# Second residual of the attention block added by TensorE in the feed-forward's bank instead of by VectorE

## The chip, the cores and the metric

One Trainium2 chip, one of its cores. The metric is the device time of one execution in microseconds (us), the median of three runs. The core's engines each work through a program of their own in order and meet by semaphores: TensorE (PE, matmuls), VectorE (DVE), ScalarE (ACT), GpSimd (POOL, which here also issues scattered DMAs) and SyncE (SP, DMA issue).

## What is computed

A transformer block on x of shape (2, 2048, 128): Performer attention with 16 heads, then a mixture of 8 experts with top-2 routing and one shared expert, each with its norms and residuals.

```python
h = _performer_attn(x, wq, wk, wv, wo, omega)
x = _layernorm(x + h, ln1_g, ln1_b)
h2 = gelu(x @ w1 + b1) @ w2 + b2
x = _layernorm(x + h2, ln2_g, ln2_b)          # the addition x + h2 is what the change moves
...
x = x + _layernorm(attention_block(_layernorm(x)))
x = x + _layernorm(experts(_layernorm(x)))     # top-2 of 8, and a shared expert
```

## The kernel before

The 4096 rows are cut into NG = 8 groups of 512 rows (n = 0 to 7; GB = 4 of them are one batch). A group lies in SBUF as 128 partitions by 4 tiles of 128 features. Three parts follow each other: attention features and the sums of the first batch (to about 175 us), a software pipeline over the eight groups (to about 404 us), and 39 blocks of expert work with a closing norm.

The change lies in the pipeline. `pipeline(stage)` makes each engine's program: for every step it goes through the groups n = 0 to 7, and group n is at its stage k = step - 2n + 5. So a group starts two steps after the one before, within a step the elder group comes first, and what an engine does for different groups is interleaved in a fixed order. A group's stages that matter here, with "(n)" for the group:

- k = 1, 2: for n >= 4 only, the division of the attention: PE turns the denominators (L698), DVE takes reciprocals (L1195), ACT spreads them (L931), PE turns them back (L705, waits for ACT), DVE multiplies (L1201, "divide"), and PE's next group of L691 waits for that.
- k = 4, 5: first residual (L1205), statistics, and first norm N1 (L1088 into MID) on DVE; PE turns N1 into the bank pT (L592).
- k = 6: ACT makes X1T = g * N1T + b on the turned side (L990, with the gains per partition). DVE makes the same x2 = g * N1 + b + b2 on the unturned side with two steps (L1255, L1257) into XN.
- k = 7: PE up projection (L778), ACT gelu (L995).
- k = 8: PE down projection into the bank pQKV, "down(n)" (L785, 16 matmuls, each of two passes). It waits for s_r2 of the group before, that is for DVE's L1275 having read the bank.
- k = 9: DVE adds x2 and the bank into R2 (L1275), takes statistics (L1077, L1081) from R2; POOL makes 1/sqrt and -mean times that (L437, L441, L503, L506).
- k = 10, 12: ACT normalises, "norm2(n)" out of R2 and then "norm3(n)" out of the result NY (both L970, four of 128 x 128 each).
- k = 11, 13, 14: DVE gain and bias (L1281, L1283), residual (L1288), last norm "norm4(n)" (L1088 into PL), of which ACT makes a copy (L986).
- k = 15 to 19: routing; k = 20, 21: POOL scatters the group's rows to DRAM with 8 indirect DMAs (L489). In its order the first of them stands behind the L506 of norm2(5).
- k = 23 to 27: the shared expert, which uses pQKV too.

What stands behind what on the in-order engines matters: in step 2n+3, PE has (in this order) down(n), turn back of the reciprocals of group n+3, the sums L691 of group n+4; and ACT has the copy L986 of group n-3, norm3(n-2), norm2(n-1) and X1T(n+1).

Of the kernel before, what the change touches and what calls it, by code (L numbers as in the profile page):

```python
# [38 lines left out]
ALU = mybir.AluOpType  # L39
# [3 lines left out]
P = 128  # L43
# [36 lines left out]
def build(nc, xs, ys, x, wqkv, wqkT, omT, wo, cols, rows, w1, w2, ew1T, ew2T, gwT, out):  # L80
# [4 lines left out]
    with ExitStack() as ctx:  # L85
# [15 lines left out]
        WH = sb("WH", [P, WA], F32R)  # L101
        WL = sb("WL", [P, WA], F32R)
        wo_s = sb("wo_s", [P, P])
        cols_s = sb("cols_s", [P, 2 + FC])
        rows_s = sb("rows_s", [P, 5, P])
        b12 = sb("b12", [P, P])
        w1_s = sb("w1_s", [P, FF])
        w2_s = sb("w2_s", [P, FC, P])
        gwT_s = sb("gwT_s", [P, E])
# [36 lines left out]
        ATX = sb("ATX", [P, 2, GW])  # L146
        ATT, X1T = ATX[:, 0, :], ATX[:, 1, :]
        MID = sb("MID", [P, 5, GW])
        N1, R2 = (MID[:, i, :] for i in range(1, 3))
        NY = [MID[:, 3, :], MID[:, 4, :]]  # L150
        HT = sb("HT", [P, FC, GW])
        XFH = sb("XFH", [P, GB, GW], F16)
# [56 lines left out]
        def parts(flat, *widths):  # L209
# [49 lines left out]
        s_num, s_nb, s_dt, s_rd = sem("den_num"), sem("den_num_copied"), sem("den_turned"), sem("den_recip")  # L259
        s_rdx, s_rx, s_att, s_wo, s_r1 = (  # L260
            sem("recip_spread"), sem("recip_turned"), sem("attn"), sem("wo_done"), sem("res1"))
        s_nT, s_x1t, s_up, s_ge, s_dn, s_r2 = (sem(n) for n in (
            "n1_turned", "x1t", "up_done", "gelu_done", "down_done", "res2"))
        s_n2g, s_y2, s_x1 = sem("n2_times_g"), sem("y_ready"), sem("x1_ready")
        s_fT, s_xft, s_xfh, s_xfl, s_lg, s_lgc = (sem(n) for n in (
            "xf_turned", "xf_copied", "xf_hi", "xf_lo", "logits", "logits_copied"))
# [3 lines left out]
        s_rt, s_place, s_base, s_slot = (sem(n) for n in (  # L270
            "routed", "placing_step", "base_next", "slots"))
        s_scat = [sem(f"scattered{g}") for g in range(GB)]
        s_n1g, s_x2 = sem("n1_times_g"), sem("x2_ready")
        s_free, s_spare = sem("rows_sent"), sem("spare_written")
        s_tab, s_fil, s_fill = sem("table_step"), sem("filler_rows_step"), sem("fillers_written")
        s_ssq, s_sc = sem("w1_squares_summed"), sem("scale_step")
# [60 lines left out]
        @block.sync  # L337
        def _(sp):
            sp.dma_start(X[:, 0, :], x_v[0]).then_inc(s_x[0], 16)
            sp.dma_start(omT_s, omT).then_inc(s_wq, 16)  # L340
            sp.dma_start(wqkT_s, wqkT).then_inc(s_wq, 16)
            sp.dma_start(W_f, wqkv).then_inc(s_wq, 16)
            sp.dma_start(X[:, 1, :], x_v[1]).then_inc(s_x[1], 16)
            sp.dma_start(EW1.rearrange("p (e h) -> p e h", e=E + 1), ew1T).then_inc(s_ew1, 16)
            sp.dma_start(rows_s[:].rearrange("p v d -> p (v d)"), rows.to_broadcast([P, 5 * P])).then_inc(s_w, 16)
            sp.dma_start(cols_s[:], cols).then_inc(s_w, 16)
            sp.dma_start(gwT_s[:], gwT).then_inc(s_w, 16)
            sp.dma_start(wo_s[:], wo).then_inc(s_w, 16)
            sp.dma_start(w1_s[:], w1).then_inc(s_w, 16)
            sp.dma_start(w2_s[:], w2).then_inc(s_w, 16)  # L350
            for g in range(2, GB):
                sp.dma_start(X[:, g, :], x_v[g]).then_inc(s_x[g], 16)
            for g in range(GB):

                sp.wait_ge(s_x[g], 16)
                sp.dma_start(X[:, GB + g, :], x_v[GB + g]).then_inc(s_x[g], 16)
            sp.dma_start(E2[:], ew2T).then_inc(s_w2, 16)

            sp.wait_ge(s_fil, 2)
            for g in range(2):  # L360
                n = SPARE // 2
                sp.dma_start(xs[E * CAP + g * n:E * CAP + (g + 1) * n].rearrange("(p a) w -> p a w", p=P),
                             SPR[:, g * n // P:(g + 1) * n // P]).then_inc(s_spare, 16)
            for b in range(B):
                for m in range(E // B):

                    if b == 0:
                        sp.wait_ge(s_batch, 1)
                    else:
                        sp.wait_ge(s_el, m + 2)  # L370
                    w = ew1T[:, bass.ds(b * (E // B) + m + 1, 1), :].rearrange("p e h -> p (e h)")
                    sp.dma_start(W1S[:, m, :], w).then_inc(s_stage[m], 16)

            sp.wait_ge(s_fil, 4)
            sp.wait_ge(s_tab, 2)
            for e in range(E):
                row = sp.value_load(filslot[0:1, e:e + 1], min_val=0, max_val=XROWS - BW)
                sp.dma_start(xs[bass.ds(row, BW)].rearrange("(p a) w -> p a w", a=2), FIL[:, e]).then_inc(s_fill, 16)

            sp.wait_ge(s_fill, 16 * E)  # L380
            for g in range(GB):
# [12 lines left out]

            for n in range(NG):
                sp.dma_start(YC[n], ys_v[n]).then_inc(s_bx[n], 16)
# [3 lines left out]
        def _(pool):  # L400
# [132 lines left out]
            rstd(0, 1)  # L533
            eng.memset(PL[:].rearrange("p g t a w -> p (g t a) w")[:, :, D:RW], 0.0).then_inc(s_free, 1)
            pool.wait_ge(s_w, 16 * NLOADS)
            eng.tensor_tensor(b12[:], rows_s[:, 1, :], rows_s[:, 2, :], ALU.add).then_inc(s_const, 1)
            pool.wait_ge(s_const, NCONST + 1)
            pool.wait_ge(s_prep_v, NPREP)
            n = SPARE // 2
# [42 lines left out]
        def _(pe):  # L582
# [170 lines left out]
            def stage(n, g, k):  # L753
# [14 lines left out]
                if k == 5:  # L768
                    pe.wait_ge(s_no[1], n + 1)

                    wait(pe, s_x1t, n)
                    turn(pT, lambda t: N1[:, t * P:(t + 1) * P]).then_inc(s_nT, 1)
                if k == 7:
                    pe.wait_ge(s_x1t, n + 1)
# [3 lines left out]
                        nc.tensor.matmul(pPK[c % 2][:], w1_s[:, c * P:(c + 1) * P], X1T,  # L778
                                         start=True, stop=True).then_inc(s_up, 1)
                if k == 8:  # L780
                    wait(pe, s_r2, n)
                    pe.wait_ge(s_ge, (n + 1) * FC)
                    for t in range(T):
                        for c in range(FC):
                            m = nc.tensor.matmul(pQKV[:, t * P:(t + 1) * P], HT[:, c, t * P:(t + 1) * P],  # L785
                                                 w2_s[:, c, :], start=(c == 0), stop=(c == FC - 1))
                    m.then_inc(s_dn, 1)
                if k == 15:
                    pe.wait_ge(s_no[4], n + 1)
# [33 lines left out]
                              [XFH[:, g], XFL[:, g]]).then_inc(s_su, 1)  # L823
                if k == SHARED + 3:

                    pe.wait_ge(*((s_sh, n) if n else (s_r2, NG)))
# [63 lines left out]
        def _(act):  # L890
# [83 lines left out]
            def stage(n, g, k):  # L974
                if k == 10:
                    if n >= 2:
                        act.wait_ge(s_x1, n - 1)
                    norm_act(2, n, R2)
                if k == 12:
                    norm_act(3, n, NY[n % 2])  # L980
                if k == 1 and n >= GB:
# [5 lines left out]
                if k == 6:  # L987
                    wait(act, s_up, n * FC)
                    act.wait_ge(s_nT, n + 1)
                    A(X1T, pT[:], ACT.Identity, scale=cols_s[:, 0:1], bias=cols_s[:, 1:2]).then_inc(s_x1t, 1)  # L990
                if k == 7:
                    wait(act, s_dn, n)
                    for c in range(FC):
# [66 lines left out]
        def _(dve):  # L1060
# [183 lines left out]
            def stage(n, g, k):  # L1244
                if k == 5:
                    if n == 0:
                        dve.wait_ge(s_spare, 16 * 2)
                    wait(dve, s_nT, n)
                    wait(dve, s_n1g, n)
                    norm(1, n, tiles(N1), XN[:, n])  # L1250
                if k == 6:

                    dve.wait_ge(s_no[1], n + 1)
                    x2, n1 = (u.rearrange("p (t d) -> p t d", t=T) for u in (XN[:, n], N1))
                    v.tensor_tensor(x2, n1, rows_s[:, 0, :].unsqueeze(1).to_broadcast([P, T, D]), ALU.mult).then_inc(s_n1g, 1)  # L1255
# [13 lines left out]
                if k == 4 and n >= GB:  # L1269
                    res1(n, pPQ)  # L1270
                if k == 9:
                    wait(dve, s_no[2], n)
                    dve.wait_ge(s_x2, n + 1)
                    dve.wait_ge(s_dn, n + 1)
                    v.tensor_tensor(R2, pQKV[:], XN[:, n], ALU.add).then_inc(s_r2, 1)  # L1275
                    hold(s_r2, n + 1)
                    stats(2, n, R2)
                if k == 11:
                    dve.wait_ge(s_no[2], n + 1)
                    y = NY[n % 2].rearrange("p (t d) -> p t d", t=T)  # L1280
                    v.tensor_tensor(y, y, rows_s[:, 3, :].unsqueeze(1).to_broadcast([P, T, D]), ALU.mult).then_inc(s_n2g, 1)  # L1281
                    dve.wait_ge(s_n2g, n + 1)
                    v.tensor_tensor(y, y, rows_s[:, 4, :].unsqueeze(1).to_broadcast([P, T, D]), ALU.add).then_inc(s_y2, 1)  # L1283
                    hold(s_y2, n + 1, at=3)
                    stats(3, n, NY[n % 2])
                if k == 13:
# [191 lines left out]
```

## Time and profile before

| what | value |
|---|---|
| median of 3 runs | 598.88 us (595.96 to 599.67) |
| the profiled execution | 594.31 us, span of its instructions 592.6 us |
| PE busy | 460.4 us (78%) |
| DVE busy | 316.1 us (53%) |
| ACT busy | 261.4 us (44%) |
| POOL busy | 245.2 us (41%) |
| chain that ended last | PE 58%, DVE 14%, POOL 8%, issue 7%, ACT 5% |

Busy shares are averages over parts with different limits; the second table of the page cuts the span into 40 slices of 14.8 us, and a digit is the busy share in tenths. The pipeline is slices 12 to 27.

### The profile page before, as it was taken

How to read it: one execution, taken by the hardware profiler on the slowest of the kernel's cores; microseconds unless marked ns; L12 is line 12 of the kernel's file. 1: busy time of each engine (PE TensorE's matmuls, PEld its weight loads, DVE VectorE, ACT ScalarE, POOL GpSimd, SP SyncE). 2: the span in 40 equal slices, each digit the busy share in tenths (PEclk: the TensorE clock that was granted, in tenths of full speed). 3: DMA queues.
4: the chain of work that ended last, by engine and by line, in shares of the span. 5: the costliest groups of instructions: out<-in, count | busy, mean ns of one | idle time of the engine just before them, and what ended most of it. 6: DMA issues, size and time to landing. Idle time of an engine off the chain costs nothing.

```text
span 592.6 us, 10592 instructions
## 1 busy us (share of the span) xinstructions
PE 460.4 (78%) x3392; PEld 355.3 (60%) x3392; DVE 316.1 (53%) x1298; ACT 261.4 (44%) x540; POOL 245.2 (41%) x368
## 2 busy tenths in 40 slices
PE   3899999999979888867727657598999999997000
PEld 2577766676655555656514435377989888987000
DVE  6887785786573578799865312301322222222394
ACT  2655544445434566644734213234445444443053
POOL 7300000110001134237887775500655555656592
PEclk9999999999998999987978777788999999999555
DMA  8920010000000000000001111330222222221622
GB/s 271 359 71 19 6 32 1 2 2 1 2 0 1 0 2 1 2 1 19 28 33 43 47 55 37 102 83 1 69 82 74 73 74 73 77 65 38 244 108 88
DMA packets 17843, 33.88 MB, mean 57 GB/s; under 512 B 4128, under 2 KB 10528, under 8 KB 17536
## 3 DMA queue, kind: packets, MB, share of 16 engines
q1 hardware_dynamic: 12096, 21.68, 11.4%
q0 software_dynamic: 4544, 9.45, 4.8%
q10 hardware_dynamic: 1152, 2.10, 0.9%
q8 instruction: 29, 0.48, 0.3%
q14 instruction: 22, 0.18, 0.1%
HBM read 19.65 MB, written 13.56 MB: 56 GB/s over the span
## 4 chain that ended last, share of the span: by engine, by line
PE 58%; DVE 14%; POOL 8%; issue 7%; ACT 5%; another core or an unknown queue 4%; DMA 2%; SPq 0%; POOLq 0%; DVEq 0%; ACTq 0%
PE pQKV L869 6%; PE pF L587 5%; POOL xs L489 4%; PE pPK L585 3%; PE pPK L587 3%; PE pPK L586 3%; PE pKV L662 3%; PE pF L585 3%; PE pQKV L831 3%; PE pPQ L869 3%; PE pF L586 3%; PE pQKV L785 2%; PE pPK L778 2%; PE pF L691 2%
## 5 line engine op out<-in xcount | busy, mean ns | idle before, releaser
L437 POOL TENSOR_TENSOR ve<-mv,eps 128x4 f32<-128x4 f32 x40 | 9.5, 238 | 209.3 <-DVE mv L1081 208.9
L556 POOL DMA_INDIRECT ys<-MID,PQT x78 | 76.0, 974 | 24.8 <-issue 24.8
L489 POOL DMA_INDIRECT xs<-PL,SLOT x64 | 64.1, 1001 | 20.0 <-issue 20.0
L1395 DVE TENSOR_SCALAR MID<-pQKV,PQT 128x128 f32<-128x128 f32 x40 | 12.2, 347 | 83.6 <-remote 66.4
L441 POOL TENSOR_TENSOR rs<-ve,halves 128x4 f32<-128x4 f32 x40 | 42.5, 1061 | 3.1
L869 PE MATMUL pQKV<-E,HT 128*128 x320 | 39.1, 275 | 1.2 <-ACT HT L1037 1.2
L585 PE MATMUL pPK<-XFH,E1H 128*128 128x512 f16 x32 | 15.3, 478 | 31.6 <-ACT MID L1015 15.3
L869 PEld LDWEIGHTS pQKV<-E,HT 128*128 128x128 f32 x320 | 37.3, 192 | 1.6 <-issue 1.4
L869 PE MATMUL pPQ<-E,HT 128*128 x304 | 37.3, 276 | 0.6 <-DVE MID L1395 0.6
L430 POOL TENSOR_TENSOR held<-halves 128x1 f32<-128x1 f32 x47 | 9.2, 195 | 67.7 <-DVE MID L1395 57.9
L869 PEld LDWEIGHTS pPQ<-E,HT 128*128 128x128 f32 x304 | 35.5, 192 | 1.2 <-issue 0.9
L778 PE MATMUL pPK<-ATX,w_s 128*128 128x512 f32 x64 | 32.9, 641 | 3.6 <-ACT HT L995 1.8
L1153 DVE TENSOR_REDUCE MX<-pPK 128x16 f32<-128x512 f32 x32 | 21.8, 682 | 24.7 <-PE pPK L587 24.6
L785 PE MATMUL pQKV<-w_s,HT 128*128 128x128 f32 x256 | 33.5, 294 | 0.3 <-ACT HT L995 0.3
L785 PEld LDWEIGHTS pQKV<-w_s,HT 128*128 128x128 f32 x256 | 32.2, 208 | 0.6 <-ACT HT L995 0.6
L995 ACT ACTIVATE HT<-pPK,cols_s 128x512 f32<-128x512 f32 x32 | 21.8, 689 | 21.9 <-PE pPK L778 20.9
L1027 ACT ACTIVATE PK<-pKV 128x256 f16<-128x256 f32 x19 | 7.3, 384 | 54.3 <-PE pF L587 47.8
L1037 ACT ACTIVATE HT<-pPK,wunscale 128x512 f32<-128x512 f32 x38 | 24.8, 687 | 11.7 <-PE pPK L587 8.6
L1387 DVE TENSOR_TENSOR PK<-pT,PK 128x256 f16<-128x256 f32 x20 | 8.5, 425 | 37.8 <-ACT PK L1027 37.5
L909 ACT ACTIVATE PK<-pPK 128x512 f32<-128x512 f32 x32 | 19.2, 600 | 20.4 <-PE pPK L645 20.4
L585 PEld LDWEIGHTS pPK<-XFH,E1H 128*128 128x128 f16 x32 | 3.8, 119 | 40.5 <-ACT MID L1015 16.8
L1037 ACT ACTIVATE HT<-pF,wunscale 128x512 f32<-128x512 f32 x40 | 25.4, 687 | 5.1 <-PE pF L587 5.1
(258 smaller groups left out, 1302.3 us busy)
## 6 DMA issues: line engine op xcount, KB each, us to landing
PQT<-xs SPq DMA_DIRECT2D x39, 132.0 KB
PQT<-in_ew1T SPq DMA_DIRECT2D x1, 2304.0 KB, 9.7
E<-in_ew2T SPq DMA_DIRECT2D x1, 2304.0 KB, 9.9
X<-in_x SPq DMA_DIRECT2D x8, 256.0 KB, 6.8
HT<-in_ew1T SPq DMA_DIRECT2D x8, 256.0 KB, 4.3
PQT<-ys SPq DMA_DIRECT2D x4, 512.0 KB
ys<-MID,PQT POOLq DMA_INDIRECT x78
xs<-PQT SPq DMA_DIRECT2D x8, 132.0 KB
```

Of the source, the lines that this page charges most:

```text
L441: eng.tensor_tensor(rs[:, j, g, :], ve[:, j, g, :], halves[:], ALU.pow).then_inc(s_rs[j], 1)
L489: eng.indirect_dma_start(xs, bass.IndirectOffsetOnAxis(SLOT[:, g, t, a:a + 1], 0), PL[:, g, t, a, :], None).then_inc(s_scat[g], 16)
L556: eng.indirect_dma_start(ys, bass.IndirectOffsetOnAxis(XS[q][:, t, ID_AT:ID_AT + 1].bitcast(U32), 0), Y[q][:, t, :], None).then_inc(s_ysc[ ...
L585: nc.tensor.matmul(o, a[0], b_[0], start=True, stop=False)
L586: nc.tensor.matmul(o, a[0], b_[1], start=False, stop=False)
L587: return nc.tensor.matmul(o, a[1], b_[0], start=False, stop=stop)
L778: nc.tensor.matmul(pPK[c % 2][:], w1_s[:, c * P:(c + 1) * P], X1T, start=True, stop=True).then_inc(s_up, 1)
L785: m = nc.tensor.matmul(pQKV[:, t * P:(t + 1) * P], HT[:, c, t * P:(t + 1) * P], w2_s[:, c, :], start=(c == 0), stop=(c == FC - 1))
L869: m = nc.tensor.matmul(outs[k % 2][:, t * P:(t + 1) * P], h[:, c, t * P:(t + 1) * P], w[c], start=(c == 0), stop=(c == EC - 1))
L995: A(HT[:, c, :], pPK[c % 2][:], ACT.Gelu, bias=cols_s[:, 2 + c:3 + c]).then_inc(s_ge, 1)
L1037: A(HT[:, k % 2 * 2 + h, :], banks[k % 2 * 2 + h][:], ACT.Silu, scale=wunscale[:]).then_inc(s_si, 1)
L1153: v.tensor_reduce(MX[:, i % 2, 1, :], pPK[i % 2][:].rearrange("p (h m) -> p h m", m=M), AX_X, ALU.max).then_inc(s_mxk, 1)
```

## The change

The feed-forward's residual x2 is no longer made by DVE. ACT makes it on the turned side, as X2T = g * N1T + (b + b2), from the bank pT right behind X1T. PE adds it into pQKV by four matmuls against the identity, one in front of each of the four accumulation groups of down(n). DVE's statistics and ACT's norm2 then read pQKV directly. DVE's L1255, L1257 and L1275 are gone, with the memset behind L1275. Three waits are new or different:

- down(n) waits for `s_no[2]`, that norm2(n-1) on ACT has been done, where it waited for `s_r2`, DVE's L1275;
- X2T(n) waits for `s_dn`, that down(n-1) has read the only X2T tile;
- PE's turn into pT waits for X2T.

The constant b + b2 becomes a column, and the loaded rows shrink from five to two.

```diff
@@ PE, stage
                 if k == 5:
                     pe.wait_ge(s_no[1], n + 1)
-                    wait(pe, s_x1t, n)
+                    wait(pe, s_x2t, n)
                     turn(pT, lambda t: N1[:, t * P:(t + 1) * P]).then_inc(s_nT, 1)
                 if k == 8:
-                    wait(pe, s_r2, n)
+                    wait(pe, s_no[2], n)
+                    pe.wait_ge(s_x2t, n + 1)
                     pe.wait_ge(s_ge, (n + 1) * FC)
                     for t in range(T):
+                        nc.tensor.matmul(pQKV[:, t * P:(t + 1) * P], X2T[:, t * P:(t + 1) * P], ident[:],
+                                         start=True, stop=False)
                         for c in range(FC):
                             m = nc.tensor.matmul(pQKV[:, t * P:(t + 1) * P], HT[:, c, t * P:(t + 1) * P],
-                                                 w2_s[:, c, :], start=(c == 0), stop=(c == FC - 1))
+                                                 w2_s[:, c, :], start=False, stop=(c == FC - 1))
@@ ACT, stage
                 if k == 10:
-                    norm_act(2, n, R2)
+                    norm_act(2, n, pQKV)
                 if k == 6:
                     A(X1T, pT[:], ACT.Identity, scale=cols_s[:, 0:1], bias=cols_s[:, 1:2]).then_inc(s_x1t, 1)
+                    wait(act, s_dn, n)
+                    A(X2T, pT[:], ACT.Identity, scale=cols_s[:, 0:1], bias=b12[:]).then_inc(s_x2t, 1)
@@ DVE, stage
                 if k == 5:
                     wait(dve, s_nT, n)
-                    wait(dve, s_n1g, n)
                     norm(1, n, tiles(N1), XN[:, n])
-                if k == 6:
-                    dve.wait_ge(s_no[1], n + 1)
-                    x2, n1 = (u.rearrange("p (t d) -> p t d", t=T) for u in (XN[:, n], N1))
-                    v.tensor_tensor(x2, n1, rows_s[:, 0, :].unsqueeze(1).to_broadcast([P, T, D]), ALU.mult).then_inc(s_n1g, 1)
-                    dve.wait_ge(s_n1g, n + 1)
-                    v.tensor_tensor(x2, x2, b12[:].unsqueeze(1).to_broadcast([P, T, D]), ALU.add).then_inc(s_x2, 1)
                 if k == 9:
-                    wait(dve, s_no[2], n)
-                    dve.wait_ge(s_x2, n + 1)
                     dve.wait_ge(s_dn, n + 1)
-                    v.tensor_tensor(R2, pQKV[:], XN[:, n], ALU.add).then_inc(s_r2, 1)
-                    hold(s_r2, n + 1)
-                    stats(2, n, R2)
+                    stats(2, n, pQKV)
```

Two places in the order. First TensorE, around down(4), in step 11 of the pipeline (L698 turns the denominators of group 7, L797 is a small routing product, L705 the turn back of group 7's reciprocals). Before:

```order
691 L698 MATMUL pF<-headpick,DEN 128x16 [waits den_num_copied]
692 L698 MATMUL pF<-headpick,DEN 128x16 x3
693 L797 MATMUL pF<-gwT_s,SQ 128x8 [waits den_num_copied,xf_copied]
694 L797 MATMUL pF<-gwT_s,SQ 128x8 x3
695 L785 MATMUL pQKV<-w_s,HT 128x128 [waits gelu_done,res2]
696 L785 MATMUL pQKV<-w_s,HT 128x128 x15
697 L705 MATMUL pF<-ident,RDX 128x128 [waits recip_spread]
```

The same place on TensorE with the change (X2T lies in MID, so the new matmuls read `ident,MID`):

```order
715 L698 MATMUL pF<-headpick,DEN 128x16 [waits den_num_copied]
716 L698 MATMUL pF<-headpick,DEN 128x16 x3
717 L800 MATMUL pF<-gwT_s,SQ 128x8 [waits den_num_copied,xf_copied]
718 L800 MATMUL pF<-gwT_s,SQ 128x8 x3
719 L785 MATMUL pQKV<-ident,MID 128x128 [waits gelu_done,x2_turned,normed2]
720 L788 MATMUL pQKV<-w_s,HT 128x128 x4
721 L785 MATMUL pQKV<-ident,MID 128x128
722 L788 MATMUL pQKV<-w_s,HT 128x128 x4
```

The place of down(4) has not moved; its first instruction waits for `normed2` instead of `res2`, and a matmul stands in front of each four.

Second, ScalarE in the same step, before the change (L970 first for norm3(2), then for norm2(3)):

```order
203 L931 ACTIVATE RDX<-RD 128x512 [waits den_recip]
204 L986 ACTIVATE PL<-PL 128x4x128 [waits normed4]
205 L970 ACTIVATE MID<-MID,nm,rs 128x128 [waits rstd3]
206 L970 ACTIVATE MID<-MID,nm,rs 128x128 x3
207 L970 ACTIVATE MID<-MID,nm,rs 128x128 [waits rstd2,x1_ready]
208 L970 ACTIVATE MID<-MID,nm,rs 128x128 x3
209 L990 ACTIVATE ATX<-pT,cols_s 128x512 [waits n1_turned,up_done]
```

And with the change:

```order
208 L934 ACTIVATE RDX<-RD 128x512 [waits den_recip]
209 L989 ACTIVATE PL<-PL 128x4x128 [waits normed4]
210 L973 ACTIVATE MID<-MID,nm,rs 128x128 [waits rstd3]
211 L973 ACTIVATE MID<-MID,nm,rs 128x128 x3
212 L973 ACTIVATE MID<-pQKV,nm,rs 128x128 [waits rstd2,x1_ready]
213 L973 ACTIVATE MID<-pQKV,nm,rs 128x128 x3
214 L993 ACTIVATE ATX<-pT,cols_s 128x512 [waits n1_turned,up_done]
215 L995 ACTIVATE MID<-pT,b,cols_s 128x512 [waits down_done]
```

The norms keep their place, behind the spreading of the reciprocals and behind the copy L986, which waits for DVE's norm4; what is new is the second reading of pT, with its wait for `down_done`.

## Rows read from the trace of the kernel before

**Rows 1.** The page's 40 slices, the rows of PE, DVE and POOL.

```profile
PE   3899999999979888867727657598999999997000
DVE  6887785786573578799865312301322222222394
POOL 7300000110001134237887775500655555656592
```

**Rows 2.** Timeline (start us, us, engine, line, what, [idle before]), POOL.

```profile
273.60 1.83 POOL L489 DMA_INDIRECT xs<-PL,SLOT  x1 [0.44 <-issue]
...
288.11 0.20 POOL L437 TENSOR_TENSOR ve<-mv,eps 128x4 f32<-128x4 f32 x1
...
381.36 0.96 POOL L489 DMA_INDIRECT xs<-PL,SLOT  x1 [0.30 <-issue]
```

**Rows 3.** Timeline of PE: the down projections and the turns behind them.

```profile
195.92 3.82 PE L785 MATMUL pQKV<-w_s,HT 128*128 128x128 f32 x32
...
209.54 3.82 PE L785 MATMUL pQKV<-w_s,HT 128*128 128x128 f32 x32
...
213.20 1.06 PE L705 MATMUL pF<-ident,RDX 128*128 128x128 f32 x8
...
224.75 3.82 PE L785 MATMUL pQKV<-w_s,HT 128*128 128x128 f32 x32
...
228.40 1.06 PE L705 MATMUL pF<-ident,RDX 128*128 128x128 f32 x8
...
240.93 3.82 PE L785 MATMUL pQKV<-w_s,HT 128*128 128x128 f32 x32
...
260.27 3.82 PE L785 MATMUL pQKV<-w_s,HT 128*128 128x128 f32 x32
```

**Rows 4.** Timeline of ACT: norm3 and norm2, and what stands around them.

```profile
197.31 1.63 ACT L970 ACTIVATE MID<-MID,nm,rs 128x128 f32<-128x128 f32 x4
...
210.93 3.18 ACT L970 ACTIVATE MID<-MID,nm,rs 128x128 f32<-128x128 f32 x8
...
227.07 3.17 ACT L970 ACTIVATE MID<-MID,nm,rs 128x128 f32<-128x128 f32 x8
...
242.45 0.63 ACT L986 ACTIVATE PL<-PL 128x512 f32<-128x512 f32 x1 [0.94 <-DVE PL L1088]
...
242.98 3.17 ACT L970 ACTIVATE MID<-MID,nm,rs 128x128 f32<-128x128 f32 x8
...
246.06 0.76 ACT L990 ACTIVATE ATX<-pT,cols_s 128x512 f32<-128x512 f32 x1
...
258.58 3.17 ACT L970 ACTIVATE MID<-MID,nm,rs 128x128 f32<-128x128 f32 x8
```

**Rows 5.** Timeline of DVE: divides, and the steps that go.

```profile
200.72 0.69 DVE L1201 TENSOR_TENSOR ATX<-pF,NUM 128x512 f32<-128x512 f32 x1 [2.72 <-PE pF L705]
...
214.35 0.69 DVE L1201 TENSOR_TENSOR ATX<-pF,NUM 128x512 f32<-128x512 f32 x1 [0.79 <-issue]
...
229.67 0.66 DVE L1201 TENSOR_TENSOR ATX<-pF,NUM 128x512 f32<-128x512 f32 x1
...
245.73 0.69 DVE L1201 TENSOR_TENSOR ATX<-pF,NUM 128x512 f32<-128x512 f32 x1
...
257.93 0.68 DVE L1255 TENSOR_TENSOR XN<-MID,rows_s 128x512 f32<-128x512 f32 x1
...
258.65 0.69 DVE L1257 TENSOR_TENSOR XN<-XN,b 128x512 f32<-128x512 f32 x1
...
268.97 0.66 DVE L1275 TENSOR_TENSOR MID<-pQKV,XN 128x512 f32<-128x512 f32 x1
```

**Rows 6.** PE by stretches: us, busy (instructions), granted clock, DMA share, GB/s.

```profile
251.60:256.30 4.70, 0.00 (x0) 0.99 0.00 0
...
256.40:259.70 3.30, 3.30 (x23) 0.52 0.00 0
...
273.40:280.20 6.80, 6.80 (x34) 0.51 0.10 32
```

More of the change, by code:

```diff
@@ L103, in build @@
         wo_s = sb("wo_s", [P, P])
-        cols_s = sb("cols_s", [P, 2 + FC])
-        rows_s = sb("rows_s", [P, 5, P])
-        b12 = sb("b12", [P, P])
+        cols_s = sb("cols_s", [P, 3 + FC])
+        rows_s = sb("rows_s", [P, 2, P])
+        b12 = sb("b12", [P, 1])
         w1_s = sb("w1_s", [P, FF])
@@ L148, in build @@
         MID = sb("MID", [P, 5, GW])
-        N1, R2 = (MID[:, i, :] for i in range(1, 3))
+        N1, X2T = (MID[:, i, :] for i in range(1, 3))
         NY = [MID[:, 3, :], MID[:, 4, :]]
@@ L261, in build @@
             sem("recip_spread"), sem("recip_turned"), sem("attn"), sem("wo_done"), sem("res1"))
-        s_nT, s_x1t, s_up, s_ge, s_dn, s_r2 = (sem(n) for n in (
-            "n1_turned", "x1t", "up_done", "gelu_done", "down_done", "res2"))
+        s_nT, s_x1t, s_up, s_ge, s_dn = (sem(n) for n in (
+            "n1_turned", "x1t", "up_done", "gelu_done", "down_done"))
         s_n2g, s_y2, s_x1 = sem("n2_times_g"), sem("y_ready"), sem("x1_ready")
@@ L272, in build @@
         s_scat = [sem(f"scattered{g}") for g in range(GB)]
-        s_n1g, s_x2 = sem("n1_times_g"), sem("x2_ready")
+        s_x2t = sem("x2_turned")
         s_free, s_spare = sem("rows_sent"), sem("spare_written")
@@ L344, in _ @@
             sp.dma_start(EW1.rearrange("p (e h) -> p e h", e=E + 1), ew1T).then_inc(s_ew1, 16)
-            sp.dma_start(rows_s[:].rearrange("p v d -> p (v d)"), rows.to_broadcast([P, 5 * P])).then_inc(s_w, 16)
+            sp.dma_start(rows_s[:].rearrange("p v d -> p (v d)"), rows.to_broadcast([P, 2 * P])).then_inc(s_w, 16)
             sp.dma_start(cols_s[:], cols).then_inc(s_w, 16)
@@ L535, in _ @@
             pool.wait_ge(s_w, 16 * NLOADS)
-            eng.tensor_tensor(b12[:], rows_s[:, 1, :], rows_s[:, 2, :], ALU.add).then_inc(s_const, 1)
+            eng.tensor_tensor(b12[:], cols_s[:, 1:2], cols_s[:, 2 + FC:3 + FC], ALU.add).then_inc(s_const, 1)
             pool.wait_ge(s_const, NCONST + 1)
@@ L824, in stage @@
                 if k == SHARED + 3:
-                    pe.wait_ge(*((s_sh, n) if n else (s_r2, NG)))
+                    pe.wait_ge(*((s_sh, n) if n else (s_no[2], NG)))
                     pe.wait_ge(s_w2, 16)
@@ L1280, in stage @@
                     y = NY[n % 2].rearrange("p (t d) -> p t d", t=T)
-                    v.tensor_tensor(y, y, rows_s[:, 3, :].unsqueeze(1).to_broadcast([P, T, D]), ALU.mult).then_inc(s_n2g, 1)
+                    v.tensor_tensor(y, y, rows_s[:, 0, :].unsqueeze(1).to_broadcast([P, T, D]), ALU.mult).then_inc(s_n2g, 1)
                     dve.wait_ge(s_n2g, n + 1)
-                    v.tensor_tensor(y, y, rows_s[:, 4, :].unsqueeze(1).to_broadcast([P, T, D]), ALU.add).then_inc(s_y2, 1)
+                    v.tensor_tensor(y, y, rows_s[:, 1, :].unsqueeze(1).to_broadcast([P, T, D]), ALU.add).then_inc(s_y2, 1)
                     hold(s_y2, n + 1, at=3)
@@ L1455 @@
         "cols": np.concatenate([f("L0_attn_ln1_g")[:, None], f("L0_attn_ln1_b")[:, None],
-                                f("L0_attn_b1").reshape(FC, P).T], axis=1),
-        "rows": np.concatenate([f(f"L0_attn_{n}") for n in ("ln1_g", "ln1_b", "b2", "ln2_g", "ln2_b")])[None, :],
+                                f("L0_attn_b1").reshape(FC, P).T, f("L0_attn_b2")[:, None]], axis=1),
+        "rows": np.concatenate([f(f"L0_attn_{n}") for n in ("ln2_g", "ln2_b")])[None, :],
         "w1": f("L0_attn_w1"),
```

## The prediction

> **What bounds the kernel now.** I read the slices first [rows 1]: the pipeline is the 13th to 27th digit (slices of 14.8 us). PE stands at 9, 8, 8, 8, 8 up to 252 us, DVE at 7, 8, 7, 9, 9 from 207 to 281 us, and POOL at 7, 8, 8, 7, 7, 7, 5, 5 from 266 to 385 us. So the pipeline has a first half in which PE and DVE hand work to each other, and a second half that is POOL's. Then I read POOL's timeline for the seam [rows 2]: the first scatter starts at 273.60, directly behind its small steps for norm2(5), the last ends at 382.32. A scatter takes 0.96 and 0.30 of issue; 64 of them are 81 us of these 109, with the small steps of the norms between them. The expert blocks need all of them. What delays the first scatter therefore delays the end one for one, and what happens to PE, ACT or DVE behind it is mostly covered. The question is what the change does to the time of POOL's steps for norm2(5).
>
> The third view is the timelines of PE, ACT and DVE up to there. They show [rows 3, 4] that down(n) on PE starts long before norm2(n-1) on ACT is through. Before the change this costs nothing: down(n) needs only DVE's L1275 of the group before. The change makes down(n) wait for exactly this norm2(n-1), since it now reads the bank that down(n) writes.
>
> **The change part by part.**
>
> *DVE loses work.* L1255 and L1257 are 0.68 and 0.69 [rows 5], about 1.3 from start to start; L1275 is 0.66, with its memset 0.7. That is 2.0 per group, 16 us over eight. It counts only where DVE sets the pace.
>
> *PE gains work.* Eight more passes per group. 32 passes of the same size take 3.82 [rows 3], 0.12 each, so 0.95 per group, on the path of down(n).
>
> *ACT gains work.* X2T is an instruction like X1T, 0.76 [rows 4]. X1T comes first and starts the up projection, so X2T is not in front of it. X2T(n+1) waits for down(n), and on ACT the routing copies and gelu(n+1) are queued behind it; all of these need PE work that comes after down(n) (the reciprocals' turn, the sums L691 at 16 passes, then the up projection), which takes more than 0.76. I cost it at nothing; if that cover were gone it would be 0.76 per group.
>
> *Statistics and norm from PSUM.* No row shows DVE statistics from a bank. DVE's nearest are L1201 (reads a bank, 0.66 to 0.69) and L1255 (does not, 0.68): 0 to 0.03 per instruction, 0 to 0.12 per group. For ACT the nearest are L990 (a bank, 0.76) and L986 (SBUF, no gain or bias, 0.63): at most 0.13 either way per instruction, 0.5 per group. I take 0 for both, as the DVE rows are alike; the ends are -2 and +2.5 over four groups. The Trainium skill (VectorE: DVE Perf Modes, the TRN2 errata) gives ScalarE a smaller and VectorE a larger fixed cost from PSUM, 52 cycles less and 62 more; by it, as an estimate, a group would have 0.17 less on ACT and 0.26 more on DVE, which no row here shows.
>
> *The new wait.* How late is norm2(n-1) for down(n)? End of ACT's L970 group minus start of L785 [rows 3, 4]:
>
> - n = 1: 198.94 - 195.92 = 3.0
> - n = 2: 214.11 - 209.54 = 4.6
> - n = 3: 230.24 - 224.75 = 5.5
> - n = 4: 246.15 - 240.93 = 5.2
> - n = 5: 261.75 - 260.27 = 1.5
>
> The norm cannot come earlier: it stands on ACT behind the reciprocals' spreading and behind the copy L986, which waited for DVE's norm4 (242.45, 0.94 idle) [rows 4]; both hang on PE's L698 just in front of down(n). All of that keeps its distance to L698, so the lateness is a true delay each time and does not wash out.
>
> Who is queued behind down(n) on PE? The turn of the reciprocals (L705), for which DVE's divide waits, and for the divide the sums L691 and the next up projection wait. In rows: divide(4) was idle 2.72 for L705; L705 of group 5 ends at 214.26 and its divide starts at 214.35; L705 of group 6 ends at 229.46 and its divide starts at 229.67 [rows 3, 5]. So the whole delay passes into DVE's divide, but for 0.2 at group 6. Hence the sum, as the shift of the divide that follows down(n):
>
> - down(0) is 0.95 longer: +0.95
> - n = 1: + 3.0 + 0.95 = 4.9
> - n = 2: + 4.6 + 0.95 = 10.4
> - n = 3: + 5.5 + 0.95 - 0.2 of slack - 0.7 (the chain divide, statistics, norm1, turn ran through DVE and has lost L1275) = 15.9
> - n = 4: + 5.2 + 0.95 - 0.2 - 0.7 = 21.2. The divides were 16.1 apart (229.67, 245.73); they would be 21.3.
> - from there to the statistics of group 5 DVE sets the pace. Two L1275 (0.7 each) and one pair L1255, L1257 (1.3) are gone: - 2.7 = 18.5
>
> down(5) is also held, by 1.5 + 0.95, but it ended at 264.09 and its L1275 came at 268.97 [rows 3, 5], 4.9 later, of which DVE's saving takes 2.0: covered. A held down(6) and down(7) have POOL's scatters as cover: POOL takes the statistics of group 6 only at 288.11 [rows 2].
>
> *TensorE's clock.* Each hold leaves PE idle for about 3.0, 4.6, 5.5 and 5.2 us. After 4.70 idle the granted clock was 0.52 for 3.3 us, that is 1.2 GHz of 2.4; after the idle before 272 us it was 0.51 for 6.8 us [rows 6]. In 3.3 us at half clock 1.65 us of work is lost, in 6.8 us 3.4. I take 1.7 for each of n = 2, 3, 4 and nothing for n = 1: + 5.1. The ends are 0 and 4 x 3.4 = 13.6. The Trainium skill (TensorE: Matmul & The Clock Gate, What's actually happening) says that an idle array falls to half clock and only activity releases it; the trace agrees, with its 0.52 after idle, and by that rule the term is not nothing but the 5.1 or more.
>
> Sum: 18.5 + 5.1 = 23.6 behind the first scatter's start, carried to the end. On the profiled execution, 594.31 + 23.6 = 617.9. The median of the runs shown is 4.6 above that execution (598.88), so the forecast for the median is 598.9 + 23.6 = **622.5 us**.
>
> **The rivals.**
>
> *The wait is free and the pieces cancel (no change).* If norm2(n-1) were through before PE reaches down(n), the sum above without its latenesses is 0.95 + 0.95 + 0.95 + 0.05 + 0.05 - 2.7, about 0.3: 599.2. It decides where the latenesses are zero. Against it: five positive numbers out of five, and the order of ACT keeps them. 5 in 100.
>
> *DVE's relief wins (faster).* As before, and PE's 0.95 lies in its own idle time besides, so that nothing of it passes to the divides. Then DVE's part counts from about 219 us on, where its digit goes to 8, 7, 9 and 9: four L1275 and three pairs before the first scatter, 4 x 0.7 + 3 x 1.3 = 6.7 less: 592.2. For it: DVE is the fullest engine just ahead of the seam. Against it: divide(4) and the next one waited for PE, not for DVE's own work [rows 5]. 5 in 100.
>
> *The delay is given back in the scatter phase.* 109 us minus 64 x 1.26 leaves 28, of which the small steps take about 20; some 8 to 10 are waits. If those vanish since the other engines are further ahead, the shift is about 14: 612. For it: the routing has more time. Against it: the waits hang on the scatters' own progress. 15 in 100.
>
> *A cold TensorE all the way.* Half clock for 6.8 us after every hold, n = 1 too: 18.5 + 13.6 = 32: 631. The half clock would also make the up projection late for its gelus. 15 in 100.
>
> The forecast itself, 617 to 628, has 60 in 100.
>
> **How the numbers follow.** A measurement of this kernel can tell about 1% from no change, 6 us. The likeliest case gives 622.5. From 607 (the delay partly given back and ACT faster from PSUM) to 634 (cold, with the PSUM costs) leaves out the two cases at or below 599 and the far ends. Slower by over 1%: 60 + 15 + 15 and less a little of the low end, 0.90; within 1% 0.05; faster 0.05.
>
> **What would show it.** In the profile after: L785 with a wait on ACT's L973 (the norm's new line) of 3 to 6 us in four groups, the largest new wait of PE; the divides about 21 us apart or more where they were 15.3 and 16.1; granted clock at half in the down projections between 210 and 270 us; the first scatter at 292 to 300; the last about 109 after it; DVE's busy sum lower by 16, PE's higher by about 8. Wrong would be: a first scatter before 280 (then the wait is free), or one at 297 with an end below 610 (given back). What would make it wrong is a norm2 that gets ahead of L698's followers, or a PE that was never the carrier of the divide.

## The result, and the profile after

The changed kernel takes 629.53 us, median of four runs (627.57 to 631.80), against 597.92 for the kernel before (four runs, 595.96 to 599.67): a ratio of 1.053, 95% interval 1.048 to 1.058. It is 31.6 us slower. The forecast was 622.5 with a range of 607 to 634: direction and place were right, the time was 7 us short and the loss 8 us short (23.6 against 31.6). The ratios in this document leave out three runs that took over 1.5% more than the fastest run of their kernel (635.45 in experiment two, 607.79 in experiment five, 606.20 of the kernel before); the medians have them in. The profiled execution of the changed kernel is the one of 627.57, with a span of 625.8 us, 33.2 over the span of before.

The page of the changed kernel, its 40 slices (15.6 us each) as in [rows 1], and the granted clock:

```profile
PE   4899999999977786677874773768999999998000
DVE  5887768677521442748763731300222222222294
POOL 7200001010001221314787675630455556556492
PEclk9999999999997987986888895779999999999555
```

In the first half of the pipeline, from about 205 to 266 us, PE reads 7, 8, 6, 6 (digits 14 to 17) where it read 8, 8, 8, 6 (digits 15 to 18 before), and DVE 4, 4, 2, 7 where it read 7, 8, 7, 9: they are not busier, they wait. Over the whole span DVE's sum has fallen from 316.1 to 297.2 us, PE's has risen from 460.4 to 478.7, ACT's from 261.4 to 264.6. Of PE's 18.3 more, 7.6 are the new passes (eight times 0.95); the rest is no work that the change adds. The new work is small; most of the time is in waiting.

The waits of PE between 184 and 300 us (who waited for whom: us in total, times, longest):

```profile
PE pQKV L785 <- ACT MID L973: 18.7, 5, 5.2
PE pT L592 <- DVE MID L1093: 5.5, 3, 4.1
PE pF L691 <- DVE ATX L1206: 2.5, 3, 0.8
```

L785 is now the first matmul of down(n), L973 is norm2. Five waits, 18.7 us: the largest on PE and one that [rows 3] did not have. PE's timeline at the first and the third of them (start us, us, engine, line, what, idle before):

```profile
195.00 1.07 PE L698 MATMUL pF<-headpick,DEN 128*128 128x16 f32 x8 [0.92 <-ACT DEN L928]
198.84 0.80 PE L785 MATMUL pQKV<-ident,MID 128*128 128x128 f32 x2 [2.78 <-ACT MID L973]
...
236.66 0.96 PE L698 MATMUL pF<-headpick,DEN 128*128 128x16 f32 x8
242.85 0.79 PE L785 MATMUL pQKV<-ident,MID 128*128 128x128 f32 x2 [5.24 <-ACT MID L973]
243.44 1.92 PE L788 MATMUL pQKV<-w_s,HT 128*128 128x128 f32 x8
...
249.01 1.06 PE L788 MATMUL pQKV<-w_s,HT 128*128 128x128 f32 x8
249.90 1.06 PE L705 MATMUL pF<-ident,RDX 128*128 128x128 f32 x8
251.80 1.92 PE L691 MATMUL pF<-PQT,KZ 128*32 128x512 f32 x16 [0.84 <-DVE ATX L1206]
```

What releases it, on ACT (L989 is the copy, the first L973 norm3, the second norm2, out of the bank):

```profile
239.25 0.63 ACT L989 ACTIVATE PL<-PL 128x512 f32<-128x512 f32 x1 [0.30 <-DVE PL L1093]
239.79 1.63 ACT L973 ACTIVATE MID<-MID,nm,rs 128x128 f32<-128x128 f32 x4
241.32 1.48 ACT L973 ACTIVATE MID<-pQKV,nm,rs 128x128 f32<-128x128 f32 x4
```

Norm2 ends at 242.80 and PE goes at 242.85. From there the delay goes the way the prediction drew: L705, the divide, L691. The divides (L1206) start at 206.87, 227.78, 251.05 and 274.95, where [rows 5] had 200.72, 214.35, 229.67 and 245.73. The last of them:

```profile
274.95 0.69 DVE L1206 TENSOR_TENSOR ATX<-pF,NUM 128x512 f32<-128x512 f32 x1 [9.90 <-issue]
```

The seam to POOL's half, and its last scatter, to set beside [rows 2]:

```profile
301.62 1.23 POOL L489 DMA_INDIRECT xs<-PL,SLOT  x1 [0.44 <-issue]
...
412.82 0.96 POOL L489 DMA_INDIRECT xs<-PL,SLOT  x1 [0.30 <-issue]
```

The first scatter is 28.0 late, the last 31.5, the end of the span 33.2. So 28 us are lost ahead of the scatters and some 5 behind their start.

The profiled executions do not all reach the pipeline at the same time, so the experiments below are compared from the start of down(0) to the first scatter. Down(0) before, and in the changed kernel:

```profile
184.08 3.84 PE L785 MATMUL pQKV<-w_s,HT 128*128 128x128 f32 x32 [0.34 <-ACT HT L995]
```

```profile
183.21 0.46 PE L785 MATMUL pQKV<-ident,MID 128*128 128x128 f32 x2 [0.43 <-ACT HT L1000]
```

That is 89.5 us before and 118.4 with the change, 28.9 more.

PE's clock in the down projections of groups 1 to 5 (us, busy, granted clock, DMA share, GB/s):

```profile
198.80:203.60 4.80, 4.76 (x22) 0.50 0.01 3
...
220.10:223.90 3.80, 3.76 (x17) 0.50 0.00 0
242.80:248.50 5.70, 5.65 (x28) 0.54 0.00 0
266.70:272.40 5.70, 5.63 (x28) 0.54 0.00 0
290.20:296.20 6.00, 5.97 (x29) 0.53 0.01 3
```

All five begin at the lower of the two levels, 1.2 GHz of 2.4. Before, down(1) to down(4) ran at a granted clock of 1.00, 3.8 us each [rows 3].

### The profile page after: what moved, and what is told of

Read it like the earlier page. It is cut to its first block, busy times and chain, and to the rows that moved or that the text cites. A ratio compares the mean times of both kernels' runs of the same rounds, so it can differ in the third digit from the quotient of the medians.

```text
span 625.8 us, 10689 instructions
## 1 busy us (share of the span) xinstructions
PE 478.7 (76%) x3456; PEld 375.0 (60%) x3456; DVE 297.2 (47%) x1266; ACT 264.6 (42%) x548; POOL 245.1 (39%) x368
## 4 chain that ended last, share of the span: by engine, by line
PE 57%; DVE 13%; ACT 9%; issue 9%; another core or an unknown queue 8%; POOL 2%; DMA 2%; SPq 0%; POOLq 0%; DVEq 0%; ACTq 0%
PE pPQ L872 6%; PE pPK L587 6%; PE pPK L585 3%; PE pQKV L788 3%; PE pPK L586 3%; PE pF L585 3%; PE pKV L662 3%; PE pF L587 3%; PE pF L586 3%; PE pPK L778 2%; ACT MID L973 2%; PE pQKV L834 2%; PE pF L691 2%; PE pQKV L872 2%
## 5 line engine op out<-in xcount | busy, mean ns | idle before, releaser
L1388 DVE TENSOR_SCALAR MID<-pPQ,PQT 128x128 f32<-128x128 f32 x38 | 11.6, 346 | 82.4 <-remote 68.2
L788 PE MATMUL pQKV<-w_s,HT 128*128 128x128 f32 x256 | 45.3, 336 | 0.0
L788 PEld LDWEIGHTS pQKV<-w_s,HT 128*128 128x128 f32 x256 | 43.2, 254 | 0.0
L785 PE MATMUL pQKV<-ident,MID 128*128 128x128 f32 x64 | 17.9, 374 | 25.0 <-ACT MID L973 24.5
L778 PE MATMUL pPK<-ATX,w_s 128*128 128x512 f32 x64 | 31.3, 612 | 4.9 <-ACT HT L1000 4.0
L1032 ACT ACTIVATE PK<-pT 128x256 f16<-128x256 f32 x20 | 7.7, 384 | 56.3 <-PE pPK L587 54.3
L785 PEld LDWEIGHTS pQKV<-ident,MID 128*128 128x128 f32 x64 | 13.8, 267 | 25.8 <-ACT MID L973 25.2
```

Of the source, the lines that this page charges most:

```text
L785: nc.tensor.matmul(pQKV[:, t * P:(t + 1) * P], X2T[:, t * P:(t + 1) * P], ident[:], start=True, stop=False)
```

## The experiments

Each was run beside the kernel before on the same chip. In the first four its median was 597.04 us, in the last four 598.27.

**One: the bank copied out by DVE.** The changed kernel with X2T and its matmuls, but the bank is free as soon as DVE has copied it.

```diff
 PE    wait for down(n):
-                    wait(pe, s_no[2], n)
+                    wait(pe, s_r2, n)
 ACT
-                    norm_act(2, n, pQKV)
+                    norm_act(2, n, R2)
 DVE, k == 9
+                    wait(dve, s_no[2], n)
                     dve.wait_ge(s_dn, n + 1)
-                    stats(2, n, pQKV)
+                    v.tensor_copy(R2, pQKV[:]).then_inc(s_r2, 1)
+                    hold(s_r2, n + 1)
+                    stats(2, n, R2)
 ... (R2 and its semaphore come back, and two waits of the shared expert follow)
```

> The changed kernel, but DVE copies the bank pQKV to SBUF once down(n) is done, statistics and norm2 read the copy, and down(n) waits for the copy instead of for norm2(n-1). X2T, its four matmuls and the loss of the two DVE steps stay. Theory A (the bank is held until ACT has normed out of it, and that alone carries the loss): the waits of PE's first matmul of down(n) on ACT's norm vanish, the divides are 13 to 16 us apart again, granted clock is full in the down projections; the four groups lose 0.95 each on PE and win 1.3 on DVE: 595 to 601 us. Theory B (the eight more passes and ACT's third use of pT carry the loss): 620 to 630, as in the changed kernel.

Measured: 604.47 us, ratio 1.014 (1.011 to 1.017). The waits on norm2 are gone, and three quarters of the loss with them: its PE waits between 184 and 300 us begin

```profile
PE pT L593 <- DVE MID L1096: 10.1, 4, 4.8
PE pPK L779 <- ACT HT L1001: 6.9, 3, 5.0
```

Theory B falls. But 601 was the upper end for theory A, and the rest is more than was allowed: 7.4 us. From the start of down(0) to the first scatter it takes 93.8 us, before 89.5: 4.3 more, which is 0.95 for each of groups 0 to 4 (4.75) with next to nothing against it. The copy stands in the place of L1275, so only the pair L1255, L1257 is gone here. DVE's timeline shows where that relief went: it has turned into waiting, in front of the divide (L1209) and of the residual (L1213):

```profile
251.94 0.69 DVE L1209 TENSOR_TENSOR ATX<-pF,NUM 128x512 f32<-128x512 f32 x1 [2.28 <-issue]
265.37 0.69 DVE L1213 TENSOR_TENSOR XN<-pPQ,XN 128x512 f32<-128x512 f32 x1 [1.15 <-PE pPQ L714]
```

The other 3 us or so lie ahead of down(0) (1.8) and behind the first scatter (1.8) in the one profiled execution; their cause is not shown.

**Two: the wait alone.** The kernel before, nothing moved, one wait added.

```diff
                 if k == 8:
                     wait(pe, s_r2, n)
+                    wait(pe, s_no[2], n)
                     pe.wait_ge(s_ge, (n + 1) * FC)
```

> The kernel before with one wait more: down(n) also waits for norm2(n-1) on ACT. No work is added, removed or moved. Theory A: PE waits 3.0, 4.6, 5.5, 5.2 and 1.5 us in groups 1 to 5, each followed by a half-clock stretch that makes the down projection about 2.3 longer; with DVE's steps still there: 598 + 18.3 + 9 = 620 to 632 us. Theory B: 597 to 602.

Measured: 629.65 us, ratio 1.052 (1.047 to 1.057): the whole loss, from a line that adds no work, with R2 still in SBUF and DVE's steps still there. PE's down(2) and down(3), idle and stretched:

```profile
220.99 5.81 PE L786 MATMUL pQKV<-w_s,HT 128*128 128x128 f32 x32 [4.50 <-issue]
...
243.77 6.34 PE L786 MATMUL pQKV<-w_s,HT 128*128 128x128 f32 x32 [5.43 <-issue]
```

In [rows 3] the same instructions took 3.82 with no such idle time. The idle time is put down to "issue" here, although the added wait is the only difference in the program: the releaser's name is not to be read alone. From down(0) to the first scatter it takes 116.8 us, 27.2 more than before and 1.7 less than in the changed kernel. So in this stretch the rest of the change (the eight passes, see six, less DVE's relief) costs about 1.7 us; in the whole time the two kernels do not differ.

**Three: two X2T tiles.** ACT waits about 6.5 us before each X2T in the changed kernel, 36.9 in six waits between 184 and 300 us. Is that a second cause?

```diff
-                    wait(act, s_dn, n)
-                    A(X2T, pT[:], ...)
+                    wait(act, s_dn, n - 1)
+                    A(X2T[n % 2], pT[:], ...)
```

> The changed kernel with two X2T tiles, so that X2T(n+1) on ACT waits for down(n-1) and not for down(n). ACT's 6.5 us waits in front of X2T go. Theory A: nothing that matters is queued behind X2T, so within 2 us of the changed kernel, 627 to 632. Theory C (ACT, blocked in X2T's wait, is late for gelu and the routing copies and so feeds the loop): 3 us or more faster, below 626.

Measured: 627.48 us, ratio 1.050 (1.047 to 1.053); 2 us under the changed kernel, with overlapping runs. ACT in that run:

```profile
242.78 0.77 ACT L993 ACTIVATE ATX<-pT,cols_s 128x512 f32<-128x512 f32 x1
243.44 0.78 ACT L995 ACTIVATE MID<-pT,b,cols_s 128x512 f32<-128x512 f32 x1
254.43 0.60 ACT L1004 ACTIVATE SQ<-pKV 128x512 f32<-128x512 f32 x1 [10.21 <-PE pKV L592]
```

X2T goes at once and the next instruction waits 10.21 for PE instead. The first scatter is at 301.71, as before that edit (301.62). ACT's longest wait costs nothing. Theory C falls.

**Four: PE kept busy in the holds.** The holds stay; PE fills them with matmuls whose results nobody uses.

```diff
                 if k == 8:
+                    if 1 <= n <= 4:
+                        pe.wait_ge(s_nb, 2 * (n + 4))
+                        for i in range((0, 2, 4, 5, 5)[n]):
+                            nc.tensor.matmul(pF[0][:, T * E:512], ident[:], w1_s[:, T * E:512],
+                                             start=True, stop=True, skip_group_check=True)
                     wait(pe, s_no[2], n)
```

> The changed kernel with 2, 4, 5 and 5 matmuls of 480 columns (results unused, into a bank that is free then) on PE ahead of down(1) to down(4), sized to fill the wait for norm2 and no more. It keeps PE busy in the holds; the holds themselves stay. Theory A with the clock as the second term: the down projections of groups 1 to 4 take 4.6 us instead of 6.5 to 7.0, the first scatter is about 9 us earlier, 619 to 622 us. Rival (the down projections are slow for another reason, such as reading X2T or the bank): down projections stay at 6.5 to 7.0, 629 us.

Measured: 618.50 us, ratio 1.035 (1.033 to 1.038), 11.0 under the changed kernel (and half a microsecond under the range) for more work on PE. Its clock in one hold and in the down projection behind it:

```profile
234.60:240.00 5.40, 4.41 (x13) 1.00 0.00 0
240.10:244.80 4.70, 4.68 (x42) 1.00 0.00 0
```

All four down projections take 4.7 us. The holds still end when norm2 does: behind its unused matmuls PE waits 0.85 to 1.11 us for it. From down(0) to the first scatter it is 109.3 us instead of 118.4: the half clock costs 9.1 us there. The rival (slow for another reason) falls. That the median moved by 11.0, two more than this, is within the spread of the two kernels' runs.

**Five: norm2 earlier on ACT.** If the loss comes from the lateness of norm2, and that from its place on ACT, moving it repairs it.

```diff
 ACT, stage
-                if k == 10:
+                if k == 10 and n > 5:
                     ...norm2(n)
                 if k == 1 and n >= GB:
                     copy_nums(n)
+                    norm2(n - GB)
                     spread_recip(n)
                 if k == 7:
                     ...gelu of the four pieces
+                    if n > GB and n - 1 <= 5:
+                        norm2(n - 1)
```

> The changed kernel with norm2(m), m = 0 to 5, moved ahead on ACT: for m = 0 to 3 between the copies of the denominators and the spreading of the reciprocals of group m + 4, for m = 4 and 5 behind gelu(m + 1); before it stood a step later behind norm3. Nothing else. Theory A (lateness of norm2, by its place on ACT): POOL's numbers for norm2 are there when ACT has copied, so down(n) has nothing to wait for, the divides are 15 to 17 apart, the clock stays full; what is left are the eight passes, 0.95 for each group, less DVE's relief: 598 to 604 us. Rival (reading the bank by ACT holds PE whatever the order): above 620.

Measured: 604.61 us, ratio 1.011 (1.007 to 1.016). ACT at group 3's place, and PE behind it:

```profile
229.55 1.51 ACT L978 ACTIVATE MID<-pQKV,nm,rs 128x128 f32<-128x128 f32 x4 [0.80 <-POOL nm L506]
230.94 0.64 ACT L934 ACTIVATE RDX<-RD 128x512 f32<-128x512 f32 x1
```

```profile
231.11 0.49 PE L785 MATMUL pQKV<-ident,MID 128*128 128x128 f32 x2 [0.95 <-ACT MID L978]
...
247.62 0.49 PE L785 MATMUL pQKV<-ident,MID 128*128 128x128 f32 x2
```

The hold has shrunk from 5.24 to 0.95, and from 4.99 to nothing, and ACT now waits for POOL's numbers. The rival falls: ACT's reading of the bank is not what costs; its place on ACT made it dear. The divides are 15.6 to 16.5 apart. But the clock does not stay full everywhere: from 197.3 to 203.3, in down(1), it is 0.72, and from down(0) to the first scatter it takes 96.9 us, 3.1 more than with the copy. At 0.6 us over its range, within the spread of its runs (598.31 to 607.79), it is, with the copy of experiment one, the best kernel with the changed arithmetic, and still 1.1% slower than the kernel before.

**Six: the passes alone.** The kernel before, with the changed kernel's extra matmuls, of zeros.

```diff
+                        nc.tensor.matmul(pQKV[:, t * P:(t + 1) * P], nil[:], ident[:], start=True, stop=False)
                         for c in range(FC):
-                            ... start=(c == 0), ...
+                            ... start=False, ...
```

> The kernel before with four more matmuls per group, of zeros against the identity, one ahead of each accumulation of down(n), the same count and shape as those that add X2T. DVE's steps and the old wait stay. If PE's time passes to the divides in full, as in the run with the copy: 0.95 for each of groups 0 to 4 and nothing later, 4 to 5 us slower, 601 to 603. If PE has idle time for them in groups 3 and 4, as the sum of the prediction had it: 2.9 us, 599 to 601.

Measured: 602.37 us, ratio 1.008 (1.005 to 1.011), 4.1 us slower. Down(0) and the first scatter:

```profile
184.46 0.49 PE L784 MATMUL pQKV<-ident,nil 128*128 128x128 f32 x2 [0.34 <-ACT HT L996]
```

```profile
278.37 1.84 POOL L489 DMA_INDIRECT xs<-PL,SLOT  x1 [0.43 <-issue]
```

That is 93.9 us, before 89.5. Counted from down(0), the divides are 1.8, 2.7, 3.5 and 4.4 later, 0.8 to 0.9 for each group: PE's added time passes to the divides nearly in full, in groups 3 and 4 too. So PE carries the first half. The 2.9 us that were set against this do not follow from the prediction's sum, though: its 0.7 a group is for the missing L1275, which this kernel has. With only the 0.2 of slack the sum gives 4.35, and that is what came.

**Seven: down(n) behind the sums.** The hold stays, but the turn of the reciprocals and L691 are put ahead of down(n) on PE.

```diff
 PE, stage
                 if k == 0 and n >= GB:
                     ...
                     num_den(n)
+                    down(n - GB)
                 if k == 2 and n >= GB:
                     turn_recip(n)
+                    if n == NG - 1:
+                        down(GB)
-                if k == 8:
+                if k == 8 and n > GB:
                     down(n), with its waits
```

> The changed kernel with another order on PE: down(0) to down(3) stand behind the turn of the reciprocals L705 and the sums L691 of group n + 4, down(4) behind the last L705. The wait for norm2 stays, and norm2 is not earlier; but what the divide needs is no longer queued behind down(n). Theory A (the loss comes by the queue behind down(n)): PE does useful work in the hold, the divides are 16 to 18 us apart instead of 21 to 24, 600 to 610 us. Rival (the held bank itself, through DVE's statistics which need down(n)): the statistics of group n are as late as before and it stays over 620.

Measured: 611.13 us, ratio 1.019 (1.013 to 1.024), 1 us over the range. Eighteen of the 32 us come back with the same wait in the program, so so it is what down(n) holds up behind it that made it dear The first scatter starts at 284.28, 17.3 earlier than in the changed kernel. (In the new place down(1) to down(3) find norm2 done and no longer wait for it, so this run does not tell a hold that is filled from a queue that is freed.) The divides are at 199.79, 218.67, 235.54 and 255.80, that is 17 to 20 apart, more than the 16 to 18 expected: L705 and the sums can now meet a cold PE themselves, here in group 6:

```profile
233.49 1.87 PE L705 MATMUL pF<-ident,RDX 128*128 128x128 f32 x8 [1.38 <-ACT RDX L940]
236.26 3.64 PE L691 MATMUL pF<-PQT,KZ 128*32 128x512 f32 x16 [0.90 <-DVE ATX L1212]
```

That is 1.87 and 3.64 us where the changed kernel took 1.06 and 1.92. In group 5 they do not (1.16 and 1.92), so this holds for some groups only.

**Eight: both moves.** Norm2 early as in five and down(n) behind the sums as in seven (the two diffs together).

> Both moves together: norm2 ahead on ACT and down(n) behind the sums L691 on PE. With norm2 early there is no hold to fill, so the order on PE should bring nothing more and only put down(n), and with it DVE's statistics, 4 us later in the step: as the run with the early norm or slower, 598 to 608 us. A time under 595 would say that the place of down(n) was a loss in the kernel before as well.

Measured: 608.61 us, ratio 1.014 (1.008 to 1.021): above the range by 0.6 us, no better than the early norm alone. No version beats the kernel before.

## Why the prediction was right, and where it was short

*The new wait.* Right. Put down: 3.0, 4.6, 5.5, 5.2 and 1.5 us late in groups 1 to 5. PE's idle time before L785: 2.78, 4.30, 5.24, 4.99 and 1.39. Norm2 is a little shorter out of the bank than out of SBUF, 1.48 against 1.63. Experiment two shows that the wait by itself makes 27.2 of the 28.9 us up to the first scatter, and the whole loss in the median.

*The way of the delay.* Right. L705 ends and the divide follows at once in each group; experiment seven, which takes L705 and L691 out of the queue behind the wait, gets 18 us back.

*The passes.* 0.95 was right (4.7 us for a down projection at full clock against 3.8). That 0.2 and 0.7 could be set against them in groups 3 and 4 was right in kind: the divides moved by 6.2, 7.3, 8.0 and 7.8 us, and hold, passes and clock give 4.3 + 0.9 + 1.9 = 7.1 for group 2, 8.5 for group 3 and 8.3 for group 4, so about 0.5 came off in each of the last two where the sum took 0.9, 0.8 too much over both.

*The clock.* Wrong in size, right in kind. The sum had 1.7 us for each of three groups, 5.1, and nothing for group 1. Measured from the start of down(n) to L705, less 4.6: 2.3, 1.9, 2.4, 2.4, so 9.0. Two things failed. Behind the idle time of 2.78 us the clock was at half as well; I had taken 3.0 to be harmless, with no row for it. And I had priced the shorter of the two cold stretches of [rows 6], where the stretches were mostly 4.8 to 6.0. The rule of the Trainium skill (TensorE: Matmul & The Clock Gate, What's actually happening), that idleness throttles and activity releases, held in every hold of the changed kernel, with 0.50 to 0.54 behind each; experiment four puts the price at 9.1 us. This term, 3.9 us, is the larger part of what the sum missed up to the first scatter (28.9 counted from down(0), against 23.6). The passes add 0.8 (above), the next point adds 1.5, and holds a little shorter than put down (17.3 against 18.3 over groups 1 to 4) take 1.0 off: 5.2 of the 5.3. Against the clock of the profile the miss looks smaller, 28.0 to 23.6, because down(0) happened to start 0.9 earlier in the profiled execution of the changed kernel.

*DVE's relief between the last divide and the first scatter.* Put down as 2.7, measured 27.87 - 26.67 = 1.2. The step that failed is that DVE sets the pace from the last divide on. Two waits for PE stand there in the changed kernel, 0.38 for L713 at 286.96 and 0.90 for down(5) at 297.67:

```profile
286.96 0.69 DVE L1210 TENSOR_TENSOR XN<-pPQ,XN 128x512 f32<-128x512 f32 x1 [0.38 <-PE pPQ L713]
...
297.67 0.89 DVE L1082 BATCH_NORM_STATS2 st<-pQKV 128x6 f32<-128x128 f32 x4 [0.90 <-PE pQKV L788]
```

For the first of them the kernel before had the reason in its rows: PE's L713 ended just when DVE was through with L1255 and L1257 and took up L1205.

```profile
257.21 1.91 PE L713 MATMUL pPQ<-wo_s,ATX 128*128 128x128 f32 x8
```

```profile
259.26 0.68 DVE L1205 TENSOR_TENSOR XN<-pPQ,XN 128x512 f32<-128x512 f32 x1
```

So without the pair DVE has to wait for L713, and the pair's 1.3 is worth next to nothing. Experiment one, which loses only the pair, shows it: 27.78 us from the last divide to the first scatter, before 27.87. The 1.2 are near what the two L1275 took (1.4). I had called down(5) covered, by my numbers with about 0.4 us to spare (4.9 - 2.0 - 2.5); at half clock it takes 7.2 us, and the cover was too thin.

*Nothing lost in the scatter phase.* Wrong by about 5 us in the two profiled executions. From the first scatter to the end of the span it is 324.2 us, before 319.0. POOL waits twice for DVE in the changed kernel where it did not before, 3.6 us the longer time (the first row; the second is the wait that both have, 7.1 in all before):

```profile
POOL ve L437 <- DVE mv L1086: 4.1, 2, 3.6
POOL held L430 <- DVE SLOT L1329: 6.5, 2, 3.8
```

That wait hangs on ACT, which stood still for 9.51 us ahead of its table load at 331.59 (last section). Most of the 9.51 is the held down(7): it starts at 322.13, when norm2(6) has just ended, and ends at 328.50, and ACT's next work stands behind it; before, down(7) ran at 286.93 and ACT reached its table load at 291.71 without a wait. What this does to the end is open. The kernels with the late norm2 have 324.0 to 324.7 us in this part (two, three and four), seven has 325.5, the copy and the zero passes 320.8 and 321.6; of the two with the early norm, in which down(6) and down(7) also wait, eight has 323.6 but five 316.1. A single execution was profiled of each, and the 316.1 is from the fastest run of its kernel, 6 us under the median, as the 319.0 is from the fastest of the kernel before. The medians leave less for this phase: 31.6 in all, less the 28.9 of the first half.

*Statistics and norm from the bank.* Right to cost at nothing: four statistics take 0.86 to 0.89 us from the bank; from SBUF their two rows span 208.93 to 209.79, 0.86 too. The larger fixed cost that the Trainium skill (VectorE: DVE Perf Modes, the TRN2 errata) gives VectorE for a source in PSUM does not show here; the smaller one that it gives ScalarE does, with 0.15 less over four (1.48 against 1.63) where the prediction's estimate was 0.17.

*The signs put down.* The divides are 20.9, 23.3 and 23.9 apart (about 21 or more), the half clock is there, DVE's sum is 18.9 lower (16). The first scatter, at 301.62, is behind the 292 to 300, the last 111.2 after it (109), and PE's sum is 18.3 higher (8), since the passes were counted and the half clock was not.

*The rivals and the range.* The delay was not given back, and the relief did not win. (By its own numbers the case of the delay given back is 613, not 612.) The cold-TensorE rival, put at 631 with 15 in 100, came nearer to the time than the forecast, but by another split: 9.0 for the clock and the rest in the scatter phase instead of 13.6 for the clock. The measured 629.53 is outside the 617 to 628 that had 60 in 100. That the wide range holds it is partly luck: its upper end was drawn for a colder TensorE and for costs of PSUM that did not come, and they made room for a loss in the scatter phase that the sum did not have.

## What to carry to other kernels

When a consumer is moved from a copy to the accumulation bank, price the release of the bank by the place of the last reader in its own engine's program, not by how long it reads; then list what is queued behind the producer, since that is what pays. An engine whose time is relieved gives nothing while another carries the chain, and it takes one run with the added work alone to see which. A wait put on TensorE can cost once more as half clock afterwards: here 9 us behind 17.3 us of waits, half as much again.

## What the runs showed of the hardware that was not expected

Behind an idle time of only 2.78 us on PE the clock was at half (down(1), 0.50 for 4.8 us), while a TensorE fed with unused matmuls in the same holds stayed at 1.00, at 11 us less for the kernel. The length of the idle time does not decide it alone: in experiment five down(1), down(2) and down(3) have 0.91, 0.91 and 0.95 us in front, and the granted clock is 0.72 in the first and 1.00 in the other two.

In the scatter phase ACT and DVE often stand still until just after a set of scatters has been issued. In the changed kernel the last scatter of a set starts at 328.97 and takes 0.96; ACT, for which down(7) was done at 328.50, begins 1.7 us after it ends:

```profile
331.59 1.28 ACT L1020 ACT_TABLE_LOAD   x1 [9.51 <-remote]
```

DVE resumes at 331.49 with 5.45 idle, "remote" too. The copy and the wait-only kernels have such a wait at the same table load (7.19 and 8.82 us on ACT), ending 28 to 31 us after the first scatter. The kernel before has none there, but has others: ACT resumes at 355.57, 370.58 and 384.03 after 6.33, 6.58 and 9.12 us, each 1.4 to 1.7 us after a set ends (354.17, 368.97, 382.32). Not all are alike: ACT's 13.77 us in the changed kernel end at 386.01, 0.2 before the set does. The trace shows one packet on each of the two instruction queues from 322.2 to 330, which would fit a late loading of code behind the scatters' packets; but it shows none from 364 to 371 in the kernel before, in which the 6.58 us lie. The cause was not tested and stays open.
